# A chain of deformable convolutions on one core: hats made by POOL alone, spreads in threes, and one group carried into the next chunk

## What is computed

```python
def _block(x, dc_w, dc_b, of_w, of_b, dw, db):
    h = relu(_deconv2d(x, dc_w, dc_b))
    offset = _conv2d(h, of_w, of_b, PAD)             # 18 maps: y and x offset of 9 taps
    return relu(_deform_conv2d(h, offset, dw, db))

def _bilinear_sample(x, py, px):
    y0, x0 = floor(py), floor(px)
    for dy in (0, 1):
        for dx in (0, 1):
            yi, xi = y0 + dy, x0 + dx
            wy, wx = 1 - abs(py - yi), 1 - abs(px - xi)
            valid = (yi >= 0) & (yi < H) & (xi >= 0) & (xi < W)
            out += x[:, clip(yi), clip(xi)] * (wy * wx * valid)

x = _block(x, ...0); in_prev = 0
for i in 1..3:
    in_cur = x + in_prev; x = _block(in_cur, ...i); in_prev = in_cur
x_cat = concat(x, in_module)
return _deform_conv2d(x_cat, _conv2d(x_cat, fin_off_w, fin_off_b), fin_dcn_w, fin_dcn_b)
```

## Time and profile before

| | us |
|---|---|
| median of 3 runs | 4316.48 (4312.64 to 4319.70) |
| span of the profiled execution, first to last instruction | 4314.1 |
| PE busy | 3880.1 (90%) |
| DVE busy | 2952.5 (68%) |
| ACT busy | 2786.4 (65%) |
| POOL busy | 1140.5 (26%) |
| spreads on PE (L544) | 1745.6 |
| samples on PE (L562) | 1342.7 |
| distance on ACT (L735), 320 times | 400.8 |
| clamp on DVE (L922), 320 times | 240.2 |
| split on POOL (L1103, L1105), 320 times each | 366.3 and 769.6 |

### The profile page before, as it was taken

One profiled execution on the slowest core, in us unless ns is written; L12 is line 12 of the kernel. 1 busy time (PEld: TensorE's weight loads), 2 busy tenths in 40 slices (PEclk: granted clock), 3 DMA queues, 4 the chain that ended last, 5 costly groups with the idle time before them and its releaser, 6 DMA issues.

```text
span 4314.1 us, 221726 instructions
## 1 busy us (share of the span) xinstructions
PE 3880.1 (90%) x81908; PEld 2973.5 (69%) x81908; DVE 2952.5 (68%) x5858; ACT 2786.4 (65%) x6651; POOL 1140.5 (26%) x645
## 2 busy tenths in 40 slices
PE   4998799699789879979988997998799999799998
PEld 3776577477567657756765775776577777577776
DVE  5885687488567668847856884784577774577775
ACT  2885588388478658837865883885355554255554
POOL 0441243134033214403322431331111110111111
PEclk8999899799989989989998997999799999899999
DMA  4442544344244334424424443443766664666664
GB/s 125 127 127 66 143 125 110 89 126 127 75 132 126 90 106 127 125 76 131 126 71 127 127 114 92 126 125 109 179 154 152 150 150 127 147 154 152 152 150 110
DMA packets 244838, 533.50 MB, mean 124 GB/s; under 512 B 61200, under 2 KB 151824, under 8 KB 227216
## 3 DMA queue, kind: packets, MB, share of 16 engines
q1 hardware_dynamic: 194224, 498.67, 45.0%
q10 hardware_dynamic: 50240, 29.89, 2.4%
HBM read 471.87 MB, written 56.45 MB: 122 GB/s over the span
## 4 chain that ended last, share of the span: by engine, by line
PE 68%; SPq 18%; issue 7%; ACT 2%; DMA 2%; DVE 2%; POOLq 0%; ACTq 0%; DVEq 0%; POOL 0%; PEld 0%; PEldq 0%
PE P L544 26%; PE PS L562 24%; SPq L380 9%; PE P L515 8%; PE PS L575 8%; SPq L388 8%; SPq L370 1%; PE PS L515 1%; ACT H L848 1%; DMA X<-x_dram 1%; PE P L530 1%; DVE FOFF L1032 1%; DMA VT<-ht_store 0%; DVE A L917 0%; DVE ST L1036 0%
## 5 line engine op out<-in xcount | busy, mean ns | idle before, releaser
L917 DVE TENSOR_TENSOR A<-P,YC 121x384 f32<-121x384 f32 (+1 forms) x4608 | 2311.4, 550 | 850.1 <-ACT YC L768 684.5
L544 PE MATMUL P<-HL,SEL 32*121 32x384 f16 (+1 forms) x21504 | 1745.6, 304 | 131.6 <-issue 95.3
L768 ACT ACTIVATE YC<-P 121x384 f32<-121x384 f32 (+1 forms) x4608 | 1733.9, 444 | 98.7 <-PE P L544 65.8
L544 PEld LDWEIGHTS P<-HL,SEL 32*121 32x121 f16 (+1 forms) x21504 | 1126.9, 117 | 513.9 <-issue 228.6
L562 PE MATMUL PS<-A,VT 121*32 121x80 f32 (+1 forms) x40960 | 1342.7, 250 | 51.7 <-DMA VT<-ht_store 15.5
L562 PEld LDWEIGHTS PS<-A,VT 121*32 121x32 f32 (+1 forms) x40960 | 1093.0, 117 | 354.6 <-issue 200.4
L1103 POOL CAST HL<-DIST 128x1152 f16<-128x1152 f32 x320 | 366.3, 1145 | 3066.1 <-DVE DIST L922 3043.8
L745 ACT ACTIVATE SMP<-PS 128x480 f32<-128x480 f32 (+3 forms) x1152 | 593.9, 516 | 638.2 <-PE PS L562 632.9
L1105 POOL TENSOR_TENSOR HL<-DIST,HL 128x1152 f16<-128x1152 f32 x320 | 769.6, 2405 | 58.5 <-POOL HL L1103 58.5
L735 ACT ACTIVATE DIST<-HB,CONST 128x1152 f32<-128x1152 f32 x320 | 400.8, 1252 | 231.4 <-DMA HB<-off_store 128.8
L575 PE MATMUL PS<-SMP,CW 128*64 128x128 f32 x7424 | 476.0, 277 | 5.4 <-ACT SMP L745 5.4
(11 more groups left out here) (61 smaller groups left out, 703.4 us busy)
## 6 DMA issues: line engine op xcount, KB each, us to landing
HB<-off_store SPq DMA_DIRECT2D x2560, 72.0 KB
VT<-ht_store SPq DMA_DIRECT2D x256, 512.0 KB
VT<-ht_store SPq DMA_DIRECT2D x768, 132.0 KB
VT<-ht_store SPq DMA_DIRECT2D x256, 88.0 KB
off_store<-FOFF SPq DMA_DIRECT2D x160, 128.0 KB, 2.6
H<-x_dram SPq DMA_DIRECT2D x5, 2048.0 KB, 14.6
ht_store<-A ACTq DMA_DIRECT2D x32, 256.0 KB, 3.3
ht_store<-VT ACTq DMA_DIRECT2D x32, 256.0 KB, 3.9
```

Source lines behind the costliest of these rows:

```text
L544: mm = nc.tensor.matmul(dst, SEL[q, table, 0:sh.npos], hats, start=part == 0, stop=part == 1)
L768: nc.scalar.activation(YC[0:sh.npos, g % X_SLOTS, 0:sh.size], P[0:sh.npos, g % Y_SLOTS, 0:sh.size], ACT.Copy).then_inc(y_ready, 1)
L917: return nc.vector.tensor_tensor(dst, x, y, ALU.mult)
```

## The change

- ACT's `distance` and DVE's `clamp` are gone. POOL makes, from `HB`, max(0, d + bias) into `DIST` and min of that with 2048 into a new tile `HAT` (`ramps`), and splits `HAT` as before (`split`). A ramp rises from 0 to 1 where a hat rises, and stays at 1. The tables of `SEL` hold +1 for position q and -1 for position q + 1, so the matmul takes the difference of two neighbouring ramps, which is the hat. `SEL` is no longer divided by 2048; ACT's copy of y scales by 1/2048 squared instead. The third body, which this data doesn't use, keeps its old tables in three more rows of `SEL`.
- `ramps` of a chunk waits for its offsets alone and stands right behind the split of the chunk before; `split` waits for `x_full` as before. SP's wait for `abs_done` becomes one for `ramp_done`, which the first ramp instruction raises.
- On PE the narrow steps now work in runs too, and no run is longer than three. Group 11 stands at the head of the first run of the next chunk (or batch), behind the wait for that chunk's hats; the last chunk's group 11 stands in the tail. ACT and DVE keep their order of groups.
- The origin's tables in `SEL` take four DVE instructions instead of two, with one more wait.

```diff
+        self.carries = int(self.ngr - 1 not in self.after)
...
                 def next_offsets(c, band, half):
 
-                    sp.wait_ge(abs_done, c - 1)
+                    sp.wait_ge(ramp_done, c - 1)
                     load_offsets(band, half)
...
-                def batch(c, b, half, prev, before):
-                    def spread_y(g):
-
-                        pe.wait_ge(y_ready, (c * sh.batches + b) * sh.ngr + g + 1)
+                def run(members):
+
+                    if len(members) > Y_SLOTS:
+                        run(members[:Y_SLOTS])
+                        members = members[Y_SLOTS:]
+                    for n, g, b, half in members:
+                        pe.wait_ge(y_ready, n + 1)
                         spread(sh, g, b, half, y_table, g % Y_SLOTS).then_inc(y_full, 1)
-
-                    def spread_x(g):
-
-                        pe.wait_ge(product_done, (c * sh.batches + b) * sh.ngr + g + 1)
+                    for n, g, b, half in members:
+                        pe.wait_ge(product_done, n + 1)
                         for tile, table in enumerate(x_tables):
                             mm = spread(sh, g, b, half, table, Y_SLOTS + g % X_SLOTS, sh.size * tile)
                         mm.then_inc(x_full, 1)
 
-                    for g in range(sh.ngr):
-                        if sh.kind == 0:
-                            spread_y(g)
-                            spread_x(g)
-                        elif g in sh.runs:
-
-                            for each in sh.runs[g]:
-                                spread_y(each)
-                            for each in sh.runs[g]:
-                                spread_x(each)
+                def batch(c, b, half, prev, before, carried):
+                    first = (c * sh.batches + b) * sh.ngr
+                    for g in range(sh.ngr - sh.carries):
+                        if g in sh.runs:
+                            members = [(first + each, each, b, half) for each in sh.runs[g]]
+                            if sh.runs[g][0] == 0 and sh.carries and carried is not None:
+                                members.insert(0, (first - 1, sh.ngr - 1, *carried))
+                            run(members)
...
-            def distance(band, half):
-
-                wait_alone(act, hb_full[half], 32 * IMG * (band + 1))
-                nc.scalar.activation(DIST[:, :], HB[:, half, :], ACT.Abs, bias=HAT_BIAS).then_inc(abs_done, 1)
-
...
                             nc.scalar.activation(YC[0:sh.npos, g % X_SLOTS, 0:sh.size], P[0:sh.npos, g % Y_SLOTS, 0:sh.size],
-                                                 ACT.Copy).then_inc(y_ready, 1)
-                            if sh.kind > 0 and b == 0 and g == sh.next_at and not last:
-                                next_distance(c + 1, band + half, 1 - half)
+                                                 ACT.Copy, scale=1.0 / SCALE ** 2).then_inc(y_ready, 1)
...
-                            if b == 0 and g == sh.next_at + 1 and not last:
-                                clamp(c + 1)
...
-                    counted(nc.vector.tensor_scalar(SEL[:, axis, :], REL[:, axis, :], ST[:, 34 + axis:35 + axis], 1.0 / SCALE,
-                                                    ALU.is_equal, ALU.mult))
+                    counted(nc.vector.tensor_scalar(TMP[:, axis, :], REL[:, axis, :], 1.0, ST[:, 34 + axis:35 + axis],
+                                                    ALU.subtract, ALU.is_equal))
                 chained()
+                for axis in range(2):
+                    counted(nc.vector.scalar_tensor_tensor(SEL[:, axis, :], REL[:, axis, :], ST[:, 34 + axis:35 + axis], TMP[:, axis, :],
+                                                           ALU.is_equal, ALU.subtract))
...
-            def hats(c, half):
-
-                wait_alone(pool, clamp_done, c + 1)
-                nc.gpsimd.tensor_copy(HL[:, 0, half, :], DIST[:, :]).then_inc(hat_step, 1)
-                wait_alone(pool, hat_step, c + 1)
-                nc.gpsimd.tensor_tensor(HL[:, 1, half, :], DIST[:, :], HL[:, 0, half, :], ALU.subtract).then_inc(hats_full, 1)
+            def ramps(c, band, half):
+
+                wait_alone(pool, hb_full[half], 32 * IMG * (band + 1))
+                nc.gpsimd.tensor_scalar(DIST[:, :], HB[:, half, :], RAMP_BIAS, 0.0, ALU.add, ALU.max).then_inc(ramp_done, 1)
+                wait_alone(pool, ramp_done, c + 1)
+                nc.gpsimd.tensor_scalar(HAT[:, :], DIST[:, :], SCALE, None, ALU.min).then_inc(hat_step, 1)
+                wait_alone(pool, hat_step, 2 * c + 1)
+
+            def split(c, half):
+
+                nc.gpsimd.tensor_copy(HL[:, 0, half, :], HAT[:, :]).then_inc(hat_step, 1)
+                wait_alone(pool, hat_step, 2 * c + 2)
+                nc.gpsimd.tensor_tensor(HL[:, 1, half, :], HAT[:, :], HL[:, 0, half, :], ALU.subtract).then_inc(hats_full, 1)
...
                     if before > 0:
 
+                        ramps(c, band, half)
                         wait_alone(pool, x_full, (c - 1) * sh.batches * sh.ngr + 1)
-                        hats(c, half)
+                        split(c, half)
```

More of the change, by code:

```diff
@@ L633, in body @@
                             prev = (c, band, b - 1, half)
+                            carried = (b - 1, half)
                         elif before == 0:
-                            prev = None
+                            prev = carried = None
                         else:
                             prev = (c - 1, band + half - 1, sh.batches - 1, 1 - half)
-                        batch(c, b, half, prev, before)
+                            carried = (sh.batches - 1, 1 - half)
+                        batch(c, b, half, prev, before, carried)
                 def tail():
+                    if sh.carries:
+                        run([(CHUNKS * sh.batches * sh.ngr - 1, sh.ngr - 1, sh.batches - 1, 1)])
                     if sh.lag == 2:
@@ L762, in body @@
                             n = (c * sh.batches + b) * sh.ngr + g
-                            if sh.kind == 0 and g == sh.next_at and not last:
-                                next_distance(c + 1, band + half, 1 - half)
                             act.wait_ge(y_full, n + 1)
@@ L1058, in step @@
                 flag_count[0] += 1
-                clamp(0)
                 chained()
```

40 lines of the change are left out of this document (17 added, 23 removed).

## The result

| | before | after |
|---|---|---|
| median of 4 runs each, us | 4314.56 (4312.64 to 4319.70) | 5019.35 (5009.72 to 5022.70) |
| span of the profiled execution | 4314.1 | 5020.9 |
| POOL busy | 1140.5 (26%) | 3466.6 (69%) |
| PE busy | 3880.1 (90%) | 4125.7 (82%) |
| ACT busy | 2786.4 (65%) | 2470.7 (49%) |

The ratio is 1.162, with a 95% interval from 1.161 to 1.164. The changed kernel is 705 us slower; the forecast was 4287 us.

What follows compares the result with a forecast made beforehand. Narrow chunks were taken as bound by SP's issue queue (8.55 us) just under compute (8.58). Saving 19 us in narrow and 10 in wide steps from 4314.1 gave 4285, plus 2.4 for the median: 4287 us, range 4255 to 4310.

Steps and rivals of the forecast that it cites:

- (d): POOL's two new ramp instructions: 1.145 us each, POOL's cycle 6.6 us, under 8.55, so no cost.
- rival 2: POOL becomes the bound: at 2.405 us a ramp its cycle is 9.08 us, total 4426 us; chance 0.08.
- signs of being wrong: Narrow chunks running at 7.3 us, POOL's idle time vanishing, or wide chunks moving by more than 0.3 us.
- (a): Narrow steps, distance and clamp gone: SP's queue keeps chunks at 8.55 us, so gain comes only at step ends.
- The gain at the end of a step: Chunk 29's samples start earlier: 3.98 us per first-group narrow step, 0.2 us per second-group step.
- Rival 3: Slack at the narrow steps' ends isn't collected: about 8 us or less is left, 4309 to 4316; chance 0.12.
- (b): Runs of three on PE in narrow steps: 0.1 us for each of three runs, 0.3 us a step.
- (c): Group 11 carried on PE behind the wait for the next chunk's hats, which are there long before: 0.
- Wide steps: Two PE runs per wide chunk become like the undisturbed one: 0.16 us a chunk, 10 us in total.
- rival 4: Wide steps gain more: the stretch of six groups falls by up to 0.4 us a chunk, 4261 us; chance 0.15.
- (e): ACT's scale inside the copy of y: 0, as it is the same activation.
- (f): Step's start: DVE's extra table instructions, under 1 us, and POOL's longer first hats stay hidden behind SP's issues: 0.

Runs made afterwards that it cites:

- either edit: Kernel before, with both ramps made on DVE instead of distance and clamp: 4312.30 us; or with one offset DMA per chunk instead of eight: 4314.85 us.
- POOL's fast forms: Changed kernel, POOL's first ramp a two-input add of a broadcast column, its second min and max with two constants: 4312.89 us.
- order alone: Kernel before with the new PE order, no carried group, first ramp on ACT and min on DVE: 4314.58 us.
- order and carry: Changed kernel with its runs and carried group, but first ramp on ACT and second on DVE: 4329.44 us.

## Why the prediction was wrong

**The step that failed is (d)**, the price of POOL's two ramps: I took 1.145 us for each, between bounds of 1.145 and 2.405, and they measured 4.18 and 3.13. The mechanism that followed is my second rival's, POOL as the bound, which decides from 2.1 us each. With the measured prices its own sum comes out: 7.31 + 3.55 + 0.72 = 11.58 us a cycle, 3.0 above 8.58, times 240 chunks is 720, less 10: 5024, and 5019 was measured. The cycle is right (11.56); that the total comes within 5 us is in part luck, since 57 us of the loss lie at the steps' starts, which that sum has at 0. I gave this rival 0.08 because the upper bound was the dearest POOL instruction in the trace. That no row showed a tensor-scalar on POOL was said, but two other instructions don't bound a third, and the bracket had no room above. What makes these forms slow is not shown: only their times are. The one fact that I had against the cast, that the ramp reads a column of bias, was only part of it: the second ramp reads none and took 3.13. Of the signs of being wrong that I named, the one that came is POOL's idle time vanishing.

By the page's rule beside it, 1.03 cycles an element for a short body (the Trainium skill, GPSIMD Engine Reference, section 3.1), a ramp is an estimate of 0.99 us plus dispatch. The form with two constants agrees with it (1.15 us), the other three tensor-scalar forms measured here, at 3.13 to 4.18 us, don't. Two readings beside it don't come out. The estimate of 2.5 us plus dispatch for two inputs lies above the 2.405 measured. And a price of about twice DVE's doesn't lead to rival 2: DVE's min took 0.75 us, twice that 1.5, and 3.0 + 3.55 + 0.72 = 7.3 us lies under 8.55. Measured against DVE, POOL took 4.2 times as long for the min (3.13 against 0.75) and 5.2 times for add and max (4.18 against 0.81).

**(a) SP's queue as the floor** was right. It had two bounds within 0.03 us; either edit alone gives nothing, both give 4%. Two things about it were off. Compute without distance and clamp was to take 7.2 or 7.3 us a chunk; with SP's loads out of the way the runs reach 7.67 to 7.85. And PE's samples were to wait 1.2 us a chunk for windows: between 140 and 340 us they wait 20.8 us in the run with ramps on DVE, 0.9 a chunk, and only 3.5 us in the one with POOL's fast forms. *The gain at the end of a step* was half of what I wrote. In the run with POOL's fast forms, SP's windows of chunk 29 and the samples of that chunk:

```profile
356.44 16.19 SPq L390 DMA_DIRECT2D VT<-ht_store  x12
```

```profile
362.87 1.04 PE L564 MATMUL PS<-A,VT 121*32 121x80 f32 x48
```

The samples follow 6.43 us behind the block, near the 6.15 that I took from the earlier trace rows. But the block itself starts 1.96 us later than in the earlier trace rows: SP entered its loop 1.1 us later, and the block that it shares with the first chunks took 4.62 us instead of 3.72:

```profile
105.81 4.96 SPq L390 DMA_DIRECT2D VT<-ht_store  x4
110.82 4.62 SPq L382 DMA_DIRECT2D HB<-off_store  x8
```

```profile
104.73 4.96 SPq L388 DMA_DIRECT2D VT<-ht_store  x4
109.74 3.72 SPq L380 DMA_DIRECT2D HB<-off_store  x8
```

The second fence is the kernel before. So the samples came 364.61 - 362.87 = 1.74 us earlier and not 3.98. Rival 3, the slack that isn't collected, is what remained once POOL was cured. I kept SP's placement fixed while I moved what feeds it.

**(b) Runs of three** gave 0 and not 0.3 us a step (order alone, 8.59 us, with the distance on ACT). **(c) The carry** at 0 was right under SP's floor (8.54 and 8.55 us with it) and wrong where the distance is on ACT (+0.17 us a chunk). **Wide steps:** the 0.16 us were right (0.18 with order and carry, 0.00 without the carry); rival 4's further gain isn't there. In the run with POOL's fast forms the chunks run at (4275.4 - 3855.5) / 24 = 17.50 us,

```profile
L733 ACT ACTIVATE TMP<-PS,BIAS x25: 367/367/368, 3855.5 to 4275.4; 128x128 f32<-128x128 f32 x25
```

yet the first wide step, where three chunks took 19.24 us instead of 17.76, gave it back: from its first spread to its last add it took 588.4 us, as before. What lengthened those three I haven't traced. **(e)** and **(f)** stay hidden with the fast forms, but for the 1.1 us at the loop's start, which I haven't split up. In the changed kernel (f) isn't 0: the 57 us at the narrow steps' starts are 7 us a step, where POOL's four instructions for chunk 0 take 11.4 us (89.58 to 100.94 in the first step).

## What to carry to other kernels

An instruction form that the trace doesn't show has no upper bound from other forms on the same engine: time it alone before it stands once per chunk, and try a second operation that does nothing where one operation is slow. Before an engine is relieved, look for a second bound just under the first, the issuing queue among them: here neither relief was worth anything alone, and both together gave 4 to 5%. Work moved to an engine with idle time can lose if it stands there ahead of an instruction that others wait for. Before an idle time until a landing is read as a reserve, take it by stretch: most of it lay between the steps here.

## What the runs showed of the hardware

**POOL's price hangs on the form, not on the number of operations.** Mean ns over 128x1152 f32, from the rows above:

| form on POOL | ns |
|---|---|
| tensor-scalar, min and max with two constants | 1147 to 1153 |
| cast to fp16 | 1145 |
| two-input add, second input a broadcast column | 2108 |
| two-input subtraction to fp16 | 2384 |
| tensor-scalar, min with a constant, nothing second | 3130 |
| tensor-scalar, add of a column, nothing second | 3215 |
| tensor-scalar, add of a column, max with a constant | 4182 |

The broadcast column by a two-input add is half the price of the same column as a scalar operand with a max behind it. These prices don't come from what runs beside POOL: in the changed kernel the shortest, median and longest of the 320 first ramps are 4168, 4181 and 4208 ns, and the first of them stands at 89.6 us, ahead of the sampling:

```profile
L1088 POOL TENSOR_SCALAR DIST<-HB,CONST x320: 4168/4181/4208, 89.6 to 4947.6; 128x1152 f32<-128x1152 f32 x160
```

**DVE's add into `X`, an instruction with two SBUF inputs, waits for POOL.** Undisturbed it takes 0.345 us (the median in the run with ramps on DVE and POOL), and beside the ramps of the change:

```profile
270.44 3.13 POOL L1090 TENSOR_SCALAR HAT<-DIST 128x1152 f32<-128x1152 f32 x1 [0.20 <-POOL DIST L1088]
```

```profile
270.72 2.76 DVE L901 SCALAR_TENSOR_TENSOR X<-X,CONST,TMP 128x128 f32 x1
```

It starts inside POOL's instruction and ends at 273.48, just when POOL's does (273.57). Of the 320 adds in the changed kernel 229 start inside one of POOL's instructions, and every one of them ends 0.08 to 0.10 us before it; the 88 with no POOL instruction beside them take 0.34 to 0.36 us. The product on DVE, which has one of its inputs in PSUM, kept its mean of 549 to 551 ns in every run. The Trainium skill (SBUF — State Buffer, Who interferes with whom) has this as a lock that is held for the whole instruction; these rows agree. What it costs in the total no run isolates; `X` isn't among the lines that the page of the changed kernel names for the chain of work that ended last.
